# Deformable sampling of a fused four-layer block: one-hots partly by ScalarE, the path selection and the weight residuals moved out of the sampling, the value product split three to one

## The reference, cut to what matters

```python
# L0: each of G = 4 groups has its own offsets; K2 = 9 taps; two 8-channel pieces, keys and values
out = gather(y0, x0) * (1 - wy_) * (1 - wx_) + gather(y0, x0 + 1) * (1 - wy_) * wx_ \
    + gather(y0 + 1, x0) * wy_ * (1 - wx_) + gather(y0 + 1, x0 + 1) * wy_ * wx_
deform_sample = out * mask[:, None]                 # for k and for v
attn = softmax(einsum('bgnc,bgckn->bgnk', qf, ks_))
out = einsum('bgnk,bgckn->bgnc', attn, vs_) @ w_proj + b_proj
# L1
attention = softmax(relu(pool @ reduction_kernel) @ attention_kernel / 30)
y = relu(batchnorm(conv(x, einsum('bk,khwio->bhwio', attention, conv_kernels))))
# L3, the choice of one of four paths of the mixer
y_soft = softmax(log_weights + gumbel)
y_hard = one_hot(argmax(y_soft), 4)
weights = y_hard - y_soft + y_soft
```

## Time and profile before

| | |
|---|---|
| median of three runs | 241.97 us |
| the profiled execution | 244.15 us, of which the profile's span is 242.3 us |
| mean granted TensorE clock | 0.965 |
| busy: TensorE matmul | 203.5 us (84%) |
| busy: VectorE | 174.1 us (72%) |
| busy: ScalarE | 91.6 us (38%) |
| busy: GpSimd | 46.5 us (19%) |
| one-hots of unit 1 start | 36.49 us |
| sampling ends (VectorE's last instruction of it) | 113.27 us |

### The profile page before, as it was taken

The page is one execution under the profiler, slowest core; times in us unless marked ns, Lnnn a source line. Parts: engine busy times, 40 slices in busy tenths (PEclk is TensorE's granted clock), DMA queues, the critical chain, the costliest instruction groups (busy, mean ns, idle before and its releaser), DMA issues.

```text
span 242.3 us, 6596 instructions
## 1 busy us (share of the span) xinstructions
PE 203.5 (84%) x2841; PEld 137.8 (57%) x2854; DVE 174.1 (72%) x378; ACT 91.6 (38%) x250; POOL 46.5 (19%) x64
## 2 busy tenths in 40 slices
PE   8799798499799889867797779858886987989995
PEld 2567398499798888712262446412323732644994
DVE  2699899993898998986654455689699559668201
ACT  2526973416385454530100270320498511036000
POOL 5912000060522531550002002215300000110000
PEclk9999999859999999999999995999998899999999
DMA  6550653264133600111631000000000081000000
GB/s 188 176 157 3 202 193 97 115 200 151 50 86 116 197 3 7 18 36 40 186 88 27 0 3 1 0 0 0 4 0 0 5 308 53 0 0 3 0 0 22
DMA packets 7373, 16.58 MB, mean 68 GB/s; under 512 B 3190, under 2 KB 5005, under 8 KB 6320
## 3 DMA queue, kind: packets, MB, share of 16 engines
q1 hardware_dynamic: 7200, 15.86, 21.1%
q10 hardware_dynamic: 144, 0.30, 0.3%
HBM read 15.38 MB, written 0.78 MB: 67 GB/s over the span
## 4 chain that ended last, share of the span: by engine, by line
PE 46%; DVE 32%; ACT 8%; issue 6%; POOL 4%; DMA 1%; POOLq 0%; DVEq 0%
PE ps L1454 41%; POOL arena L558 2%; DVE arena L1348 2%; POOL rstd L551 2%; DVE arena L1345 2%; DVE onehot L1006 2%; ACT indexb L659 2%; PE ps L1729 2%; DVE att L1045 2%; PE ps L1728 2%; DMA cst<-in_cst 1%; DVE dots L1027 1%; DVE comp L1312 1%; ACT indexb L614 1%; ACT pexp L681 1%
## 5 line engine op out<-in xcount | busy, mean ns | idle before, releaser
L1454 PE MATMUL ps<-spare 128*128 128x512 bf16 (+1 forms) x207 | 56.6, 400 | 12.9 <-ACT onehot L614 2.7
L1454 PE MATMUL ps<-table,onehot 128*128 128x64 bf16 x1728 | 53.8, 195 | 4.3 <-DVE onehot L1006 2.1
L1454 PEld LDWEIGHTS ps<-table,onehot 128*128 128x128 bf16 x1728 | 53.2, 99 | 5.6 <-issue 4.3
L1454 PEld LDWEIGHTS ps<-spare 128*128 128x128 bf16 x217 | 19.3, 104 | 41.2 <-issue 4.7
L433 POOL TENSOR_TENSOR arena<-arena,w4p 128x288 f32<-128x288 f32 x28 | 22.0, 816 | 65.4 <-DVE w4p L1020 65.4
L673 ACT ACTIVATE arena<-ps 128x512 f32<-128x512 f32 x36 | 21.4, 596 | 34.6 <-PE ps L1454 34.4
L1454 PE MATMUL ps<-arena 128*32 128x66 f32 (+5 forms) x380 | 24.3, 286 | 2.0 <-DVE arena L1348 1.5
L1006 DVE TENSOR_SCALAR onehot<-indexb,cst 128x2304 bf16<-128x2304 bf16 x32 | 24.6, 831 | 0.4 <-ACT indexb L659 0.4
L1454 PEld LDWEIGHTS ps<-arena 128*32 128x32 f32 (+2 forms) x380 | 21.1, 158 | 4.9 <-DVE arena L1348 2.0
L551 POOL TENSOR_TENSOR rstd<-var_eps,cst 128x4 f32<-128x4 f32 (+2 forms) x9 | 8.8, 982 | 73.0 <-DVE var_eps L887 47.0
L424 DVE TENSOR_TENSOR arena<-arena,q_tok 128x1152 f32<-128x1152 f32 x8 | 10.9, 1356 | 6.5 <-ACT arena L673 6.5
(11 more groups left out here) (285 smaller groups left out, 321.1 us busy)
## 6 DMA issues: line engine op xcount, KB each, us to landing
indexb<-index_rows SPq DMA_DIRECT2D x7, 1152.0 KB, 5.8
arena<-in_toep SPq DMA_DIRECT2D x1, 2120.5 KB, 8.0
l<-in_l SPq DMA_DIRECT2D x1, 646.5 KB
onehot<-lin_split SPq DMA_DIRECT2D x6, 96.0 KB
stu_fq<-in_stu SPq DMA_DIRECT2D x1, 560.0 KB, 3.7
table<-stu_split SPq DMA_DIRECT2D x7, 70.0 KB, 2.0
l<-in_l SPq DMA_DIRECT2D x1, 384.0 KB, 6.4
l<-in_l SPq DMA_DIRECT2D x1, 342.0 KB, 2.9
```

The costliest lines, as they stand in the source:

```text
L1454: return nc.tensor.matmul(out_ap, lhsT, rhs, start=start, stop=stop)
```

## The change

Nine pieces:

1. ScalarE makes an eighth of the one-hots of units 1 to 7: the last nine of 36 columns, second half of the table. `distances` takes |index - row| and `own_one_hots` relu(1 - |index - row|), after the first and after the second group that ScalarE copies in the unit before. VectorE's fourth one-hot instruction covers nine columns in place of eighteen. The index transfer and TensorE wait for ScalarE's part too (`s_oa`, `s_os`).
2. The sum over corners and the smallest logit of unit u - 2 stand between the one-hot instructions of unit u; before, they ended step u - 1.
3. GpSimd's value product covers three groups of four, for units 0 to 5. VectorE does the fourth right after the weights (`value_part`), and GpSimd waits for that (`part`). `w4p` has two halves in turn.
4. VectorE does all four groups of units 6 and 7 (`values_here`).
5. The value sums of units 5 and 6 are made in two parts: TensorE adds the four corners (`corners`: four fp32 matmuls of 288 columns with the identity, every fourth element of the product) and VectorE sums the nine taps (`values_from_corners`).
6. The selection: three instructions after `poolbd`, ScalarE's exponential before that of the kernel mix, the rest of the chain after `bshift`, ahead of x2. TensorE's matmuls with `wpick` stand between the convolution and the transpose of x2.
7. The mixer's scaling and splits come after y1 on ScalarE; on TensorE the subtractions stand among the spare matmuls of the layer norm, and the transpose of the norm waits for the last of them.
8. The linear attention's residuals come after the last unit, in banks 2 and 3.
9. Fewer spare matmuls: 11 after the last unit where there were 32, and 8 between the convolution and the norm's transpose where there were 17.

The diff, cut to its core:

```diff
-lin_ps, moe_ps, stu_ps = ps[:, 0:2, 0:LQ], ps[:, M_BANK, 0:2 * MQ], ps[:, S_BANK, 0:SQ]
+lin_ps, moe_ps, stu_ps = ps[:, 2:4, 0:LQ], ps[:, M_BANK, 0:2 * MQ], ps[:, S_BANK, 0:SQ]
+dense_ps = ps[:, 0, :].rearrange("p (b n) -> p b n", b=2)[:, :, 0:P]
+corner_sums = [ps[:, 4 + i, 0:J * HC] for i in range(2)]
...
+OWN = J // 4
...
+        if u >= 3:
+            sp.wait_ge(s_oa, u - 2)
...
-    for u in range(T - 1):
-        pool_e.wait_ge(v1.sem, v1[f"w4p{u}"])
-        values_product(nc.gpsimd, u).then_inc(s_pv, 1)
+    for u in range(T - 2):
+        pool_e.wait_ge(v1.sem, v1[f"part{u}"])
+        values_product(nc.gpsimd, u, range(G - 1)).then_inc(s_pv, 1)
...
+    def distances(u):
+        act.wait_ge(d_ix[u % 2], 16 * ((u + 1) // 2))
+        if u >= 2:
+            act.wait_ge(s_un, u - 1)
+        nc.scalar.activation(ohv[:, u % 2, 1, J - OWN:, :], ixb[:, u % 2, J - OWN:, :], ACT.Abs, bias=npidx[:])\
+            .then_inc(s_oa, 1)
+    def own_one_hots(u):
+        act.wait_ge(s_oa, u)
+        nc.scalar.activation(ohv[:, u % 2, 1, J - OWN:, :], ohv[:, u % 2, 1, J - OWN:, :], ACT.Relu,
+                             bias=pos1[:], scale=-1.0).then_inc(s_os, 1)
...
+        first = done
         while 8 * (done + 1) <= (u + 1) * J:
             sample_group(done)
             done += 1
-        if u == 0:
-            act.wait_ge(vz.sem, vz["zneg"])
-            nc.scalar.activation(soft[:], zsel[:], ACT.Exp, bias=zmax[:], accum_out=zsum[:])\
-                .then_inc(az.sem, az.step("exp"))
+            if u + 1 < T and done == first + 1:
+                distances(u + 1)
+            if u + 1 < T and done == first + 2:
+                own_one_hots(u + 1)
+    unit_exp(T - 2)
+    split(lin3, 1, lin_ps, "lm", "l1")
+    unit_exp(T - 1)
...
+    act.wait_ge(tw.sem, tw["sel"])
+    act.wait_ge(g0.sem, g0["sigma"])
+    for k in range(NF // 2):
+        ins = nc.scalar.activation(stu_raw[:, k * D:(k + 1) * D], stu_ps[:, k * D:(k + 1) * D], ACT.Copy,
+                                   scale=sig4[:, k:k + 1])
+    ins.then_inc(aw.sem, aw.step("scaled"))
+    copy(stu_raw[:, NF // 2 * D:], stu_ps[:, NF // 2 * D:], aw, "taps")
+    act.wait_ge(aw.sem, aw["taps"])
+    copy(stu3[:, 0, :], stu_raw[:], aw, "sh")
+    split(stu3, 1, stu_ps, "sm", "s1")
+    split(stu3, 2, stu_ps, "sl", "s2")
...
+            if q and half and u:
+                js = slice(js.start, J - OWN)
             ins = nv.tensor_scalar(ohv[:, u % 2, q, js, :], ixb[:, u % 2, js, :], c["pidx"][:, q:q + 1],
                                    None, ALU.is_equal)
+            if between:
+                between[q](u - 2)
...
+            dve.wait_ge(s_pv, min(u - 1, T - 2))
         dve.wait_ge(s_px, u + 1)
-        nv.tensor_tensor(out=w4p[:].rearrange("p (n k) -> p n k", k=4),
+        nv.tensor_tensor(out=half_of(w4p[:], u % 2).rearrange("p (n k) -> p n k", k=4),
                          in0=w4[:, u * J * 4:(u + 1) * J * 4].rearrange("p (n k) -> p n k", k=4),
                          in1=rep(pexp[:], 4), op=ALU.mult).then_inc(v1.sem, v1.step(f"w4p{u}"))
+    def value_part(u):
+        dve.wait_ge(v1.sem, v1[f"w4p{u}"])
+        values_product(nv, u, range(G - 1, G)).then_inc(v1.sem, v1.step(f"part{u}"))
...
     def last_units():
+        logits(L - 1)
+        peaks(L - 1)
         keys(L)
+        key_sums(L)
         weights(L - 1)
-        key_sums(L)
-        dve.wait_ge(s_pv, L - 1)
-        value_sums(L - 2)
+        weighted_dots(L)
         logits(L)
-        dve.wait_ge(s_pv, L)
-        value_sums(L - 1)
+        peaks(L)
+        values_here(L - 1)
+        values_from_corners(L - 2, 0)
         weights(L)
-        dve.wait_ge(v1.sem, v1[f"w4p{L}"])
-        values_product(nv, L).then_inc(v1.sem, v1.step(f"values{L}"))
+        values_here(L)
+        values_from_corners(L - 1, 1)
         dve.wait_ge(v1.sem, v1[f"values{L}"])
         value_sums(L)
...
+    def values_here(u):
+        dve.wait_ge(v1.sem, v1[f"w4p{u}"])
+        values_product(nv, u).then_inc(v1.sem, v1.step(f"values{u}"))
+    def values_from_corners(u, i):
+        b, h = u // NH, u % NH
+        dve.wait_ge(t1.sem, t1[f"corners{u}"])
+        nv.reduce_sum(tokhb(att[:])[:, h, b, :], corner_sums[i].rearrange("p (n s) -> p n s", s=K2), axis=AX.X)\
+            .then_inc(v1.sem, v1.step(f"mixed{u}"))
     nv.tensor_tensor(out=away, in0=pos, in1=near, op=ALU.subtract).then_inc(v0.sem, v0.step("away"))
     for u in range(T):
-        one_hots(u, 0)
+        one_hots(u, 0, (logits, peaks) if u >= 2 else ())
...
+    nv.tensor_tensor(out=zsel[:], in0=c["logw"], in1=c["gumbel"], op=ALU.add).then_inc(vz.sem, vz.step("z"))
+    dve.wait_ge(vz.sem, vz["z"])
+    nv.reduce_max(zmax[:], zsel[:], axis=AX.X).then_inc(vz.sem, vz.step("zmax"))
+    dve.wait_ge(vz.sem, vz["zmax"])
+    nv.tensor_scalar(zmax[:], zmax[:], -1.0, None, ALU.mult).then_inc(vz.sem, vz.step("zneg"))
...
+    dve.wait_ge(az.sem, az["exp"])
+    nv.reciprocal(zsum[:], zsum[:]).then_inc(vz.sem, vz.step("zinv"))
...
+    nv.tensor_scalar(nwpick[:], wpick[:], -1.0, None, ALU.mult).then_inc(vz.sem, vz.step("nwpick"))
     dve.wait_ge(a2.sem, a2["y1"])
     nv.tensor_tensor(out=x2, in0=x1[:], in1=y1, op=ALU.add).then_inc(v2.sem, v2.step("x2"))
...
+        elif u == "linear middle":
+            pe.wait_ge(aw.sem, aw["lh"])
+            lin_rest(1).then_inc(tw.sem, tw.step("l1"))
+        elif u == "linear low":
+            pe.wait_ge(aw.sem, aw["lm"])
+            lin_rest(2).then_inc(tw.sem, tw.step("l2"))
+        elif u == "mixer middle":
...
+                if j == J - OWN and u:
+                    pe.wait_ge(s_os, u)
...
+    def corners(u, i):
+        for k in range(4):
+            ins = mm(corner_sums[i], ident, prod_v[u % 2].rearrange("p (m k) -> p k m", k=4)[:, k], start=k == 0, stop=k == 3)
+        ins.then_inc(t1.sem, t1.step(f"corners{u}"))
     pe.wait_ge(s_ge, B * GRP)
-    occupied(4, SB[0])
-    occupied_after(v1, (f"keys{L}", 4), (f"dots{L}", 4), (f"mixed{L - 2}", 4), (f"logit{L}", 3),
-                   (f"mixed{L - 1}", 3), (f"w4p{L}", 4), (f"values{L}", 4), (f"mixed{L}", 2), bank=SB[0])
+    weights_prepared("linear middle")
+    pe.wait_ge(s_pv, T - 2)
+    corners(L - 2, 0)
+    weights_prepared("linear low")
+    occupied_after(v1, (f"peak{L}", 3), (f"w4p{L - 1}", 2), bank=6)
+    pe.wait_ge(v1.sem, v1[f"values{L - 1}"])
+    corners(L - 1, 1)
+    occupied_after(v1, (f"values{L}", 2), (f"mixed{L - 1}", 2), (f"mixed{L}", 2), bank=6)
     pe.wait_ge(v1.sem, v1["att"])
-    pe.wait_ge(aw.sem, aw["sl"])
...
-    occupied(2, 7)
+    weights_prepared("selection")
     pe.wait_ge(v2.sem, v2["x2"])
...
+    occupied_after(v3, ("cen", 3), bank=7)
+    weights_prepared("mixer middle")
+    occupied_after(v3, ("eps", 2), bank=7)
+    weights_prepared("mixer low")
+    pe.wait_ge(aw.sem, aw["sl"])
     pe.wait_ge(v3.sem, v3["ln"])
```

152 lines of the change are left out of this document (68 added, 84 removed).

## The result

The changed kernel takes 246.06 us, the median of 4 runs (245.62 to 246.22). Against the runs of the kernel before on the same chips the ratio is 1.0156, with a 95% interval of 1.0124 to 1.0188: 3.8 us slower (the medians alone differ by 4.1), where 3.5 us faster was forecast. Ratios here leave out runs over 1.5% above the fastest of their kernel, such as a fourth run of the kernel before, at 247.94 us; medians of the experiments are of all runs, which moves none of them by more than 0.2 us. The profiled execution takes 245.62 us, its span 243.8.

The account below looks back on a forecast made before the run. VectorE was taken to set the pace from the fourth unit step, TensorE being late before it. Terms -2.46 - 2.25 - 0.3 + 1.2 + 0.2 + 0.1 = -3.5 gave 238.5 us against the median, range 235.6 to 241.6.

Parts of the forecast that it names:

- The unit step: One VectorE step of the sampling, one-hots to one-hots: 8.27 us would become 7.61, -0.66 for each full step.
- steps 4 to 7: Sampling from the one-hots of unit 4 to the last keys: 35.24 us would become 32.78, -2.46.
- The weighting: VectorE's weighting of the dots: 0.56 us of each later step is a wait for GpSimd; it would cost 0.31.
- The other way: Weighting slips in between two of GpSimd's four instructions under the port lock; gain per step as small as 0.1 us.
- Before step 4: Sampling ahead of unit 4: earlier index transfer for unit 3, selection matmuls gone, one shorter step; -2.25 us.
- The rival: Sampling steps shrink less: weighting still waits, or new TensorE stops behind index transfers cost 3.3 us; 240 to 241.4, chance 0.30.
- The tail: From the last keys to the end of sampling: 11.45 us would become 11.1 to 11.2, -0.3.
- The queue: TensorE's tail order: linear middle, corner sums, linear low, five spare matmuls, corner sums; 8.6 us, each corner set 1.9.
- The bound of +2: Tail: the case of a strided read at half speed in the corner sums, +2 us.
- The convolution stage: Selection chain and matmuls delay the transpose of the convolution result, +1.2 us; mixer weights delay the norm, +0.2.
- The clock rival: TensorE's clock falls to 1.2 GHz in unit steps, two such units costing 2.7 us net: 244.7, chance 0.08.
- the first stop: TensorE's 2.82 us stop before 47.71, start of unit 2; its going was a rival worth another 4.3: 234.2, chance 0.12.

Follow-up runs that it names:

- experiment 10: The kernel of 9 with GpSimd making all four groups of the value product for units 0 to 5, VectorE none there: 239.11 us.
- Experiment 1: The changed kernel without the five index transfers for units 3 to 7, one-hots made from the indices of units 1 and 2: 238.75 us.
- 4: The changed kernel with index transfers for units 3 to 7 in three pieces, each issued when the one before has landed: 240.83 us.
- 9: The changed kernel with whole index transfers, those for units 3, 4, 5 held until TensorE has filled 6, 11, 15 groups: 244.94 us.
- experiment 2: The changed kernel with each corner-sum matmul reading 288 adjacent elements instead of every fourth of 1152 (sum of wrong elements): 242.06 us.
- experiment 8: The changed kernel with transfers in three pieces, corners of units 5 and 6 stored outermost, and the selection moved back into the sampling: 235.15 us.

## Why the prediction was wrong

**The unit step and steps 4 to 7** were right: 7.64 for 7.61, waits of 0.81 and 0.80 for 0.90, -2.3 for -2.5. The weighting was read rightly as a wait for GpSimd (0.30, and 0.86 again in experiment 10). The section "SBUF: two separate sides" of the Trainium skill's "SBUF — State Buffer" agrees with these rows. The other way it left, that the weighting slips in between two of GpSimd's instructions, does occur, in step 2 of the kernel before:

```profile
50.84 3.66 POOL L433 TENSOR_TENSOR arena<-arena,w4p 128x288 f32<-128x288 f32 x4 [31.08 <-DVE w4p L1020]
51.97 0.59 DVE L1033 TENSOR_TENSOR dots<-dots,w 128x144 f32<-128x144 f32 x1
```

It was done at 52.56, 1.94 us before GpSimd's product: it waited for the second of the four instructions, which had begun at 51.60, and for no more. In step 4 it starts just behind the start of the last of the four, and there the two ways can't be told apart. In the changed kernel it starts 0.05 us after GpSimd's product has ended (74.89, 74.84), where 0.2 was worked out; the gain held by a narrow margin.

**Before step 4 (-2.25, measured +0.9)** is one of the two steps that failed. TensorE did resume earlier, at 46.52 for a forecast 46.9. What failed is the sentence that the 3.3 us of the selection chain "fall into VectorE's own idle time and gain nothing". With them gone from VectorE's queue its later one-hots, and so the issue of the transfers for units 4 and 5, moved 3.7 and 3.8 us earlier, onto TensorE's next two fetches. Each of the first two stops ended 1.0 and 0.5 us after the next transfer went out, so each stop set up the next. The last of them cost more than itself: the granted clock was 0.50 behind it (62 to 64 us), and unit 3 took 8.01 us for 6.46. Experiment 1 shows the cause, 4 and 9 that it is what lies ahead of a fetch, and when, rather than the bytes moved. That it was the chain that moved the issues is read from the order on VectorE; no run put the chain alone back into the changed kernel. The rival had such a stop, in unit 5, at 3.3 us; the places where it costs most, in units 2 and 3, were not followed through. It came in unit 5 too (84.16, 1.24 us), with little effect. A stop elsewhere than at the start of unit 2 stood among the signs that would make the prediction wrong.

**The tail (-0.3, measured +3.9)** is the other. The queue was right, the size of one term was not: four corner matmuls are 4.05 us, not 1.9. The price was taken from a row of adjacent elements, 0.47 us for 280 columns, and the step of 16 bytes was left to a bound. The bound of +2 for a strided read at half speed counted one set where both are on the path. "Advanced Engine Details and Errata" of the Trainium skill, section "Memory Cachelines", says that operands whose every access falls in another 16-byte line of SBUF pay a penalty; the 4.05 against 1.94 us of experiment 2 agree. The page gives no factor: by its rule a price above that of the adjacent row belonged in the forecast, but not how much.

**The convolution stage** was right (+1.0 for +1.2, and experiment 8 gives it back: 5.27 for 6.31 us from the convolution to the transpose of x2). **The clock rival** did not happen in the paced steps, where idle times of TensorE alone brought no lower clock: the clock stayed at 1.00, and units 4 and 7, which had no stop, took 6.46 and 6.47 us. In this part of the kernel it was at 0.50 only behind stops, at the start of unit 2, as before, and of unit 3. So the level that the rival feared came in more than one unit, but from the stops and not from shorter steps.

By "Instruction fetch mechanics" in "Runtime: NRT & Kernel Launch" of the Trainium skill a fetch is mostly hidden and the first stop would have gone. The five stops say otherwise. Its blocks of 256 instructions fit: from 53.27 to the stop that ended at 60.56 lie 128 matmuls of two instructions each.

## What to carry to other kernels

Before work is moved off an engine that issues or releases large transfers, work out when the transfers will go, and lay them beside the long instruction stream's block boundaries: TensorE here used up 128 matmuls in about 4 us, which left no slack for a transfer of 5.9 us ahead of its fetch. In these kernels large transfers beside a busy TensorE were better issued in pieces, as far as nobody waited for the last. Price a matmul from a row with the same step between elements, and count every copy of it that the path holds.
